# A graph network's edge placement: four tiles to a comparison, the value scaled in by ScalarE

## The reference

```python
edge_index = jnp.stack([src, dst])
...
w = jnp.einsum('rb,bio->rio', att, basis)          # layer 3: 2 relations, 30 bases, 512x512
x_j = x[col]
...
msg = jnp.where((edge_type == 0)[:, None], msgs[0], msgs[1])
agg = jax.ops.segment_sum(msg, row, num_segments=x.shape[0])
```

## Time and profile before

| | |
|---|---|
| median of 3 runs | 1849.04 us (1828.67 to 1850.15) |
| profiled execution | 1847.77 us, span of its instructions 1846.0 us |
| granted TensorE clock, mean | 0.931 |
| TensorE busy | 1550.3 us (84%) |
| VectorE busy | 1150.0 us (62%) |
| ScalarE busy | 523.8 us (28%) |
| GpSimd busy | 752.3 us (41%) |
| the stage that is changed | from about 191 to 283 us of the span |

### The profile page before, as it was taken

The page is one execution under the profiler, slowest core; times in us unless marked ns, Lnnn a source line. Parts: engine busy times, 40 slices in busy tenths (PEclk is TensorE's granted clock), DMA queues, the critical chain, the costliest instruction groups (busy, mean ns, idle before and its releaser), DMA issues. The chain is left out here.

```text
span 1846.0 us, 26332 instructions
## 1 busy us (share of the span) xinstructions
PE 1550.3 (84%) x7525; PEld 922.5 (50%) x7526; DVE 1150.0 (62%) x2260; ACT 523.8 (28%) x915; POOL 752.3 (41%) x625
## 2 busy tenths in 40 slices
PE   6888795777499999967775399993988899999998
PEld 4542562334455555534444255542446446864586
DVE  6967797887467777776767766666747522113222
ACT  3302113433245555522444100001112122211221
POOL 1427776886176666483002477773220110000000
PEclk9968898999689999988997599997999999999999
DMA  4137773002866666702883277773023003200022
GB/s 146 69 117 258 243 249 83 2 1 81 306 215 193 187 187 187 131 25 115 306 341 138 71 210 210 210 206 64 0 86 80 1 0 136 67 20 1 29 72 70
DMA packets 82352, 235.93 MB, mean 128 GB/s; under 512 B 28069, under 2 KB 28950, under 8 KB 78186
## 3 DMA queue, kind: packets, MB, share of 16 engines
q0 software_dynamic: 34592, 96.87, 19.6%
q1 hardware_dynamic: 40298, 126.11, 19.2%
q10 hardware_dynamic: 7392, 12.06, 2.0%
HBM read 207.41 MB, written 27.41 MB: 127 GB/s over the span
## 5 line engine op out<-in xcount | busy, mean ns | idle before, releaser
L801 POOL DMA_INDIRECT tab_slots<-slot_words,slot_address x160 | 254.3, 1590 | 113.1 <-issue 77.9
L1556 PE MATMUL dense_pY<-weights,dense_xT_block 128*128 128x512 f32 x640 | 283.5, 600 | 0.0
L830 POOL DMA_INDIRECT e_rows<-tab_h,idx_h x176 | 178.6, 1015 | 225.6 <-POOLq L50 151.7
L1611 PE MATMUL dense_pY<-parts,dense_number 128*128 128x512 f32 x1000 | 237.9, 399 | 8.3 <-ACT dense_number L1600 8.3
L1131 POOL DMA_INDIRECT e_rows<-tab_q,idx_q x192 | 182.2, 949 | 119.1 <-PE e_pS L1204 44.1
L1611 PEld LDWEIGHTS dense_pY<-parts,dense_number 128*128 128x128 f32 x1000 | 189.0, 189 | 56.1 <-ACT dense_number L1600 9.4
L924 PE MATMUL e_pS<-e_rows,e_onehot_ring 128*128 128x512 f32 x352 | 194.7, 643 | 20.8 <-DVE e_rows L900 18.3
L1556 PEld LDWEIGHTS dense_pY<-weights,dense_xT_block 128*128 128x128 f32 x640 | 121.3, 193 | 142.9 <-issue 142.9
L1204 PE MATMUL e_pS<-e_rows,e_onehot_f 128*128 128x512 f32 x384 | 181.7, 596 | 0.0
L1014 PE MATMUL count_pA<-count_onehot_d,count_onehot_s 128*128 128x512 f16 (+1 forms) x576 | 116.2, 349 | 48.4 <-DVE count_onehot_d L992 46.6
L900 DVE TENSOR_TENSOR e_rows<-e_rows,e_pW 128x1024 f32<-128x1024 f32 x88 | 107.3, 1219 | 66.9 <-DMA e_rows<-tab_h,idx_h 66.7
(11 more groups left out here) (315 smaller groups left out, 2449.1 us busy)
## 6 DMA issues: line engine op xcount, KB each, us to landing
basis_piece<-in_L_gnn_basis_pieces SPq DMA_DIRECT2D x32, 2048.0 KB, 8.5
dense_short_number<-tab_edges_from SPq DMA_DIRECT2D x20, 640.0 KB, 3.8
tab_edges_from<-counts_turned SPq DMA_DIRECT2D x10, 640.0 KB
tab_w<-basis_wout ACTq DMA_DIRECT2D x128, 32.0 KB
weights<-tab_w SPq DMA_DIRECT2D x4, 1024.0 KB
tab_edges_to<-counts_total SPq DMA_DIRECT2D x10, 320.0 KB
dense_short_number<-tab_edges_to SPq DMA_DIRECT2D x10, 320.0 KB, 3.4
weights<-in_L_gnn_W_T SPq DMA_DIRECT2D x3, 1024.0 KB, 14.8
```

The costliest lines, as they stand in the source:

```text
L801: pool.indirect_dma_start(self.table, bass.IndirectOffsetOnAxis(self.address[:, t:t + 1], 0), self.words[:, t, :], None).then_inc(self.pla ...
L830: pool.indirect_dma_start(self.rows[:, q, s, :], None, self.table, bass.IndirectOffsetOnAxis(self.idx[:, j * 2 + s:j * 2 + s + 1], 0)).the ...
L1556: ins = self.nc.tensor.matmul(self.banks.at(g), self.xt[:, b % 2, c, :], weights[:, c, :], start=c == 0, stop=c == 3)
L1611: ins = self.nc.tensor.matmul(self.banks.at(self.first + b), self.number[:, b % 2, r * NB + k, :], self.parts[r][n][:, k, :], start=k == 0 ...
```

## The change

`onehot_s` is compared four tiles at a time, too, without the value; its ring is three batches of four. The ring of `onehot_p` gets three batches instead of four. ScalarE reads each tile of `onehot_p` from the batch and writes it, multiplied by the edge's `value` (a scale per partition, read from a tile), to a new ring `valued` of 8, which is now the stationary operand. The store of a half piece stands inside ScalarE's loop over the tiles, after tile 8n+11. All the loops of ScalarE, VectorE and TensorE are written out over the 160 tiles. Loads, products and the scatters are as before. `EVERY` is 8.

```diff
-    RING, STEP = 8, T // basis.steps
-    QUARTER = STEP // 4
-    TOGETHER, BATCHES = 4, 4
+    TOGETHER, BATCHES, SCALED = 4, 3, 8
...
-        ons = c1.enter_context(nc.sbuf_tensor(f"{name}_onehot_s", [EP, RING, slots], F32))
+        ons = c1.enter_context(nc.sbuf_tensor(f"{name}_onehot_s", [EP, BATCHES, TOGETHER, slots], F32))
+        valued = c1.enter_context(nc.sbuf_tensor(f"{name}_valued", [EP, SCALED, P], F32))
...
         @block.scalar
         def _(act):
-            def step(i):
-                for n in range(4):
-                    basis.store(act, i, n // 2, n % 2)
-            peeled(act, basis.steps, step)
+            for t in range(T):
+                if t % TOGETHER == 0:
+                    act.wait_ge(built, t // TOGETHER + 1)
+                wait(act, placed, t + 1 - SCALED)
+                nc.scalar.activation(valued[:, t % SCALED, :], onp[:, t // TOGETHER % BATCHES, t % TOGETHER, :], ACT.Copy,
+                                     scale=value[:, t:t + 1]).then_inc(scaled, 1)
+                if t % EVERY == 3 and t > EVERY:
+                    n = t // EVERY - 1
+                    basis.store(act, n // 4, n // 2 % 2, n % 2)
+            n = T // EVERY - 1
+            basis.store(act, n // 4, n // 2 % 2, n % 2)
             basis.end_store(act)

         @block.vector
         def _(v):
-            def step(i):
-                for u in range(STEP):
...
-                    wait(v, placed, i * STEP + (u + 1 - RING))
-                    nc.vector.tensor_scalar(ons[:, k, :], C.f("iota_slot", EP)[:, 0:slots], pos_s[:, bass.ds(t, 1)],
-                                            value[:, bass.ds(t, 1)], ALU.is_equal, ALU.mult).then_inc(built, 1)
-            peeled(v, T // STEP, step)
+            for g in range(T // TOGETHER):
+                at = slice(g * TOGETHER, (g + 1) * TOGETHER)
+                wait(v, placed, (g + 1 - BATCHES) * TOGETHER)
+                nc.vector.tensor_tensor(
+                    onp[:, g % BATCHES, :, :], C.f("iota_p", EP).unsqueeze(1).to_broadcast([EP, TOGETHER, P]),
+                    pos_p[:, at].unsqueeze(2).to_broadcast([EP, TOGETHER, P]), ALU.is_equal)
+                nc.vector.tensor_tensor(
+                    ons[:, g % BATCHES, :, :], C.f("iota_slot", EP)[:, 0:slots].unsqueeze(1).to_broadcast([EP, TOGETHER, slots]),
+                    pos_s[:, at].unsqueeze(2).to_broadcast([EP, TOGETHER, slots]), ALU.is_equal).then_inc(built, 1)
             v.wait_ge(placed, T)
             nc.vector.tensor_copy(sorted_out, po[:, 0:slots])

         @block.tensor
         def _(pe):
...
+            for t in range(T):
+                pe.wait_ge(scaled, t + 1)
+                nc.tensor.matmul(po[:, 0:slots], valued[:, t % SCALED, :], ons[:, t // TOGETHER % BATCHES, t % TOGETHER, :],
+                                 start=t == 0, stop=t == T - 1).then_inc(placed, 1)
+                if t % EVERY == EVERY - 1:
+                    n = t // EVERY
+                    if n == 0:
+                        basis.start_multiply(pe)
+                    basis.multiply(pe, n // 4, n // 2 % 2, n % 2)
```

More of the change, by code:

```diff
@@ L726, in place_edges @@
         onp = c1.enter_context(nc.sbuf_tensor(f"{name}_onehot_p", [EP, BATCHES, TOGETHER, P], F32))
-        ons = c1.enter_context(nc.sbuf_tensor(f"{name}_onehot_s", [EP, RING, slots], F32))
+        ons = c1.enter_context(nc.sbuf_tensor(f"{name}_onehot_s", [EP, BATCHES, TOGETHER, slots], F32))
+        valued = c1.enter_context(nc.sbuf_tensor(f"{name}_valued", [EP, SCALED, P], F32))
         po = c1.enter_context(nc.psum_tensor(f"{name}_pO", [P, D], F32))
-        built, placed = sem("built"), sem("placed")
+        built, scaled, placed = sem("built"), sem("scaled"), sem("placed")
         basis.begin(c1, sem)
+        EVERY = T // (basis.steps * 4)
         block = c1.enter_context(nc.Block())
```

## The result

The changed kernel took 1855.2 us in the median of 20 runs (1840.07 to 1865.16), the kernel before 1846.78 us (1828.67 to 1850.15, also 20). The ratio is 1.0058, with a 95% interval of 1.0038 to 1.0079: slower by 7 to 15 us, far within 2%. The forecast was 1864 (1844 to 1880), with 0.91 for a time within 2%. The profiled execution took 1862.17 us, the third slowest of its 20, with a span of 1860.4, against 1847.77 and 1846.0 before.

What follows compares the result with a forecast made beforehand. VectorE was taken as the bound, TensorE 6% behind. Nine cycles of 9.49 us plus a first period of 4.45 give 89.9 us instead of 74.55, +15.3: 1863.1 profiled, 1864 by the median, range 1844 to 1880.

Steps and rivals of the forecast that it cites:

- the rings: VectorE's batches and ScalarE's scaled tiles: no batch would come late by a tenth that counts, so no cost.
- The gain of VectorE's part: VectorE's batch of four tiles falls from 2.00 to 1.48 us, TensorE sets the pace: 1.9 us gained in all.
- A cycle of sixteen tiles: TensorE between products of the same kind: 9.49 us instead of 7.58, nine times, 17.2 us lost.
- wrong if the waits are far from 1.9: Sign: nine TensorE waits for ScalarE's tile of about 1.9 us after odd stores; otherwise the issues' price is wrong.
- The four issues: DMA issues on ScalarE after every second store: 1.95 us, mean of ten rows running from 1.51 to 2.62.
- The first period: TensorE's first period of the stage was put at 4.45 us, the later ones without stall at 3.79.
- start and tail: Stage before the first store and after the last (copy, issues, landing, barrier): taken to stay unchanged.
- the loops written out count for nothing: Loops of TensorE, ScalarE and VectorE: no TensorE gap at the turns, slack for the added instructions, so zero.
- GpSimd: The stage's 42 scatters wait for wide comparisons and then need 1.06 us; VectorE is not held; no cost.
- (b): Rival: ScalarE bound by its rate, 1873, or VectorE's comparisons held by scatters, 1871; both together 17%.
- (a): Rival: the stall behind ScalarE's issues is hidden and TensorE sets the pace, 1847; 8%.
- (c): Rival: TensorE's clock falls to 1.2 GHz through the stalls, slower than 2%, 1913 if all stage; 6%.

Runs made afterwards that it cites:

- run 1: Changed kernel with the four DMA issues of every store moved from ScalarE to SyncE: 1845.4 us, ratio to the kernel before 0.9999, stage 89.98 us.
- run 2: Changed kernel with the store of a half piece after tile 8n+15 instead of 8n+11: 1856.28 us in its one run, stage 91.29 us.
- run 3: Changed kernel with five batches instead of three and 16 scaled tiles instead of eight, store unmoved: stage 101.78 us (changed kernel 101.26).
- run 6: Changed kernel without ScalarE's tiles and the multiplication by value, TensorE reading the batch itself: stage 89.60 us, 18 periods 69.04 us.
- run 11: Kernel before with only ScalarE's loop over the stores written out: stage 90.51 us, four issues 1.49 us in the mean against 1.95.
- run 9: Kernel before with the stage's 42 scatters moved to the counting stage: stage 88.83 us against 91.44, 18 periods 68.28 us.
- run 8: Changed kernel with the store after tile 8n+15, five batches and 16 scaled tiles: 1847.17 us, ratio to the kernel before 1.0031, stage 90.36 us.
- run 5: Changed kernel with two of each store's four DMAs issued as two halves, six issues in all: stage 113.34 us (changed kernel 101.26).
- run 4: Changed kernel with each of a store's four DMAs issued as two halves, eight issues in all: stage 135.87 us (changed kernel 101.26).

## Why the prediction was right

**The mechanism, as put.** Queued behind the stores on ScalarE, the tiles came late after every second store; nine waits, none after the even stores, the rest hidden. Runs 1, 2 and 3 show the cause, the lead of four tiles, and that the rings don't matter at this place of the store. The gain of VectorE's part was forecast at 1.9 us for the periods; that much lay above TensorE's pace (1.8), but run 6 has 1.1 of it there, for the loads of the pieces come next, which the prediction didn't look at. That its stage is 1.8 us shorter all the same is luck.

**The durations.** A product with its scale took 389 ns (forecast 380) at a pitch of (2.45-0.39)/7 = 0.29 (0.29), the wide comparison 955 ns (950). These came from slopes and differences between neighbouring shapes, and that was good enough.

**The term that was mis-sized.** A cycle of sixteen tiles took 8.94 us in the mean, not 9.49: 1.36 lost instead of 1.91, and the idle time in it was 1.06 to 1.15. By the prediction's own sign ("wrong if the waits are far from 1.9") that term was wrong. The four issues were put at 1.95 us, the mean of ten rows, and took 1.34; the gap ahead of them 0.15 and was 0.02. Against that stand about 0.1 us between the last issue and the next tile, which the sum didn't have. Nine times 0.55 is 5.0 us. The first period was 4.90 instead of 4.45, and start and tail gave back 0.96; together that is the distance between the forecast's +15.3 and the stage's +9.8.

Two steps went into the 0.6 us that the issues had too much. The first is the sentence that **the loops written out count for nothing "from both sides"**: I looked at the turns of the loops and at who has slack, and not at what a DMA issue inside a loop costs, 0.22 us of the mean (run 11). The second is that the mean of the ten rows was carried over as though it were a price. 0.4 us of it were delays beside moving pieces, and these are no property of the issues: in kernels with the loop written out the delay was 0.02 in the mean (changed), 0.17 (run 11) and 0.53 (run 2). With 1.34 for the issues the sum would have been 5.5 us less.

**What was luck.** The median of 1855.2 lies below the 1859 to 1870 of the sum and its own bounds; it is inside the range because that was widened for the spread of the runs. Of the 9 us to the forecast's 1864, 2 are that the kernel before has a median of 1846.8 and not the 1849 of its first three runs.

**GpSimd.** That scatters wait for wide comparisons was right, and cost the stage nothing: of 1.35 us in the mean instead of 1.65, they were done at 261.7 instead of 274.0. The lock as the Trainium skill states it (SBUF — State Buffer, Who interferes with whom), read as in the prediction, would have held the wide comparisons for the scatters; they took 0.95 to 1.01 us beside them. The same passage adds, marked as inferred, that a `tensor_tensor` takes only the read side of the shared pair and descriptor generation the write side; that goes with the comparisons not being held, and it should have stood beside rival (b). But the sentence that VectorE is not held by scatters was drawn from wide comparisons alone; the single ones with two scalars from tiles were slower beside scatters, by 0.24 us in four (run 9, and the last batch before). That changes how is to be read: the 2.00 us of a batch had the scatters in it, and "what bounds the kernel" was VectorE with a scatter in every batch.

**The rivals.** (a) would have needed issues of 0.04 us; the wait goes only where they are moved (run 1) or the store is placed later (runs 2 and 8). (b) is out by ScalarE's pitch and the length of the comparisons. (c) didn't come: behind every one of the nine waits the four tiles take 1.57 us, 2.4 GHz. (The mean over the whole stage, 0.94, is under the 0.95 that the prediction named as a sign, but it was 0.95 before: the slow part is the start.) It was nearer than 6% sounds: two more issues brought some of the matmuls behind the waits to 1.2 GHz (run 5), and with four more the lower clock cost more than the longer waits themselves (run 4).

**What stays open.** Why issues beside a moving piece vary from 1.32 to 2.6 us, how scatters add to that, and the 6.5 us of the profiled pair in the edge scores.

## What to carry to other kernels

When work is moved to an engine with slack, look at what else stands in its program: 12 busy microseconds of 90 don't help if the engine is away for 2 us at a time and the order of the program lets it be only 1.4 us ahead. Count how many items are ready when it goes away, and place the slow item behind as many as the ring holds (run 2), or give DMA issues to a queue with nothing behind it (run 1). Here the change bought 1.1 us on VectorE (run 6) and paid 11.4 on ScalarE (80.48 against 69.04), and the repaired versions come out even, since TensorE was only 6% behind the old bound and the loads close behind TensorE. Where an instruction's duration is read from a trace, look also at what runs beside it: the 6% that VectorE was behind TensorE came from scatters.

## What the runs showed of the hardware

- Four DMA issues on ScalarE take 1.32 us when no piece is being loaded and the addresses are constants, 1.60 in a hardware loop with computed addresses (0.16 us between two issues instead of 0.03; run 11). The price goes by number: eight halves take 2.96, 0.37 each. Beside a load they take up to 1.74 without scatters (run 9) and up to 2.62 with them (before); scatters alone don't lengthen them (1.60 at 270.83).
- GpSimd's scatters slow VectorE's `tensor_scalar` of 192 float32 values with two scalars from tiles: four took 1.48 us beside them, 1.24 without, and it is one of the four, 0.62 instead of 0.37. Two-input comparisons weren't held (0.95 to 1.01 us), and held the scatters up (1.65 us in the mean before, 1.19 undisturbed).
- After waits of TensorE of 1.84 to 2.08 us (run 5) the next four tiles ran at 2.4 GHz in six cases of seven. After the eleven waits of 2.30 to 3.14 us (runs 4 and 5) there were matmuls at 1.2 GHz every time, in nine at once and in two a little later.
